# A two-layer residual kernel whose first layer is computed by one level of Strassen, with the second layer as a phase of its own

## The reference

```python
# layer 0: one weight matrix for all, plus a gated low-rank part
base   = einsum('btd,od->bto', x, W)                  # W: 1024 x 1024
logits = einsum('btd,ed->bte', x, Wr) + 5.0 * one_hot(language_id)   # 8 experts
topw, topi = top_k(logits, 2);  weights = softmax(topw)
gates  = sum(one_hot(topi) * weights)
h      = einsum('btd,erd->bter', x, A)                # 8 experts, rank 16
x = x + base + 2.0 * einsum('bter,bte,eor->bto', h, gates, B)
# layer 1: each sequence has its own 1024 x 1024 matrix, picked by adapter id
w = weight[adapter_ids]                               # 16 matrices to pick from
x = x + einsum('bsi,boi->bso', x, w)
```

## Time and profile before

| | |
|---|---|
| median of 3 runs | 424.41 us (424.09 to 424.89) |
| profiled execution, its own time from first to last instruction (the span) | 423.0 us |
| PE busy | 414.4 us, 98% of the span |
| DVE busy | 314.1 us, 74% |
| ACT busy | 163.1 us, 39% |
| POOL busy | 59.5 us, 14% |
| DMA traffic | 68.5 MB, mean 162 GB/s |
| granted TensorE clock | 1.000 |

### The profile page before, as it was taken

One profiled execution on the slowest core, in us unless ns is written; L12 is line 12 of the kernel. 1 busy time (PEld: TensorE's weight loads), 2 busy tenths in 40 slices (PEclk: granted clock), 3 DMA queues, 4 the chain that ended last, 5 costly groups with the idle time before them and its releaser, 6 DMA issues.

```text
span 423.0 us, 6707 instructions
## 1 busy us (share of the span) xinstructions
PE 414.4 (98%) x1978; PEld 349.1 (83%) x1978; DVE 314.1 (74%) x378; ACT 163.1 (39%) x192; POOL 59.5 (14%) x104
## 2 busy tenths in 40 slices
PE   8898999999999999999999999999999999999996
PEld 8786888888898888888888888888889888888885
DVE  3999999999307999998615799999830799994410
ACT  3432544555212455454321445455421245533321
POOL 1021211201200121012110022111310012221000
PEclk9999999999999999999999999999999999999999
DMA  7994677797913666699650576679960356654111
GB/s 173 232 219 120 167 190 200 212 259 203 225 47 99 150 187 180 161 260 249 173 132 0 153 181 188 170 218 252 243 160 26 99 151 175 189 161 123 51 50 50
DMA packets 82542, 68.52 MB, mean 162 GB/s; under 512 B 7986, under 2 KB 82258, under 8 KB 82514
## 3 DMA queue, kind: packets, MB, share of 16 engines
q1 hardware_dynamic: 65618, 59.84, 55.3%
q10 hardware_dynamic: 16896, 8.39, 7.3%
HBM read 59.81 MB, written 8.39 MB: 161 GB/s over the span
## 4 chain that ended last, share of the span: by engine, by line
PE 89%; DVE 3%; DMA 2%; SPq 2%; issue 2%; ACT 0%; POOL 0%; DVEq 0%; ACTq 0%; POOLq 0%
PE banks L564 28%; PE banks L565 28%; PE banks L566 28%; PE banks L577 4%; SPq L255 2%; PE banks L579 1%; DMA raw<-in_L_cond_W_dram 1%; DMA raw<-in_x_dram 1%; DVE turned L349 1%; DVE turned L345 0%; DVE w_lo L356 0%; POOL raw L301 0%; PE gT_ps L611 0%; ACT w_hi L487 0%; DVE gT_lo L449 0%
## 5 line engine op out<-in xcount | busy, mean ns | idle before, releaser
L356 DVE TENSOR_TENSOR w_lo<-turned,w_hi 128x1024 fp32r<-128x1024 f32 x96 | 118.8, 1259 | 38.8 <-ACT w_hi L487 38.0
L487 ACT ACTIVATE w_hi<-turned 128x1024 fp32r<-128x1024 f32 x96 | 101.5, 1062 | 113.1 <-DVE turned L349 103.3
L349 DVE STREAM_TRANSPOSE turned<-raw 128x1024 f32<-128x1024 f32 x113 | 135.3, 1225 | 10.1 <-DMA raw<-in_x_dram 5.1
L301 POOL TENSOR_TENSOR raw<-raw,ident 128x128 f32<-128x128 f32 x96 | 58.4, 608 | 325.9 <-DMA raw<-in_L_cond_weight_dram 182.7
L564 PE MATMUL banks<-xT_hi,w_hi 128*128 128x512 f32 x256 | 100.2, 391 | 0.0
L565 PE MATMUL banks<-xT_lo,w_hi 128*128 128x512 f32 x256 | 99.7, 389 | 0.0
L566 PE MATMUL banks<-xT_hi,w_lo 128*128 128x512 f32 x256 | 99.6, 389 | 0.0
L564 PE MATMUL banks<-w_hi,x1T_hi 128*128 128x512 f32 x256 | 99.6, 389 | 0.0
L565 PE MATMUL banks<-w_lo,x1T_hi 128*128 128x512 f32 x256 | 99.6, 389 | 0.0
L566 PE MATMUL banks<-w_hi,x1T_lo 128*128 128x512 f32 x256 | 99.6, 389 | 0.0
L566 PEld LDWEIGHTS banks<-xT_hi,w_lo 128*128 128x128 f32 x256 | 48.1, 188 | 10.0
(11 more groups left out here) (54 smaller groups left out, 197.8 us busy)
## 6 DMA issues: line engine op xcount, KB each, us to landing
raw<-in_L_cond_weight_dram SPq DMA_DIRECT2D x256, 128.0 KB, 2.7
raw<-in_L_cond_W_dram SPq DMA_DIRECT2D x128, 128.0 KB, 3.5
raw<-in_x_dram SPq DMA_DIRECT2D x64, 128.0 KB, 3.3
out_dram<-out_stage ACTq DMA_DIRECT2D x32, 256.0 KB, 3.1
raw<-in_L_cond_A_dram SPq DMA_DIRECT2D x4, 128.0 KB, 3.1
raw<-in_L_cond_B_dram SPq DMA_DIRECT2D x4, 128.0 KB, 4.5
gated<-in_L_cond_Wr_dram SPq DMA_DIRECT2D x4, 8.0 KB
lang_i<-in_itok_B_dram SPq DMA_DIRECT2D x1, 4.0 KB, 2.9
```

Of the source, the lines that this page charges most:

```text
L301: nc.gpsimd.tensor_tensor(spot, spot, ident[:].rearrange("p (q j) -> p q j", q=Q), ALU.add)\
L349: nc.vector.transpose(turned[:, slot(item, ch, last, 2)].rearrange("p m (q s) -> p q m s", q=Q), raw[:, s, :].rearrange("p (q m j) -> p q ...
L356: nc.vector.tensor_tensor(dest(False, item), turned[:, slot(item, ch, last, 2)], dest(True, item).bitcast(F32), ALU.subtract)\
L487: nc.scalar.activation(dest(True, item), turned[:, slot(item, ch, last, 2)], ACT.Copy)\
```

## The change

**Layer 0 by Strassen.** Tokens are worked in two spans of 1024 instead of four chunks of 512. In a span, x (two halves of 512 tokens, two halves of 512 features) and W (two halves of outputs, two of features) are 2 x 2 blocks, and seven products of sums stand for eight plain ones. A round computes 4 output tiles of 128 outputs x 512 tokens: seven `product`s, each 4 steps of three matmuls with 512 columns. There are 4 rounds in a span, 8 in all. Each operand part of a product is a piece: for x a piece for each tile of tokens (`("x", span, t, i)`), for W one for each round (`("u", n, i)`), each 128 x 512. Of the seven x pieces five are sums, of the seven W pieces five are sums; POOL makes them (`add_up`) into a ring of three half tiles. Every piece is then split by ACT and DVE as before. Partial results are combined by ACT copies, three DVE instructions and one POOL add in each round, and each round ends in the eviction of 4 banks by ACT and DVE.

**Features** are computed on the turned x itself (f32, one matmul of 136 columns for each step) in place of two fp32r matmuls on its split parts. The gates are made four times, for four tiles each.

**x1 by way of DRAM.** The results of layer 0, split in high and low parts, are stored to a DRAM scratch `x1_kept` by SP (`keep_round`) and loaded back for each sequence in layer 1 (`load_x1`).

**Layer 1** runs behind all of layer 0: 8 sequences (rows), each 4 banks of 8 steps of three matmuls with 512 columns. Its 64 weight tiles come through a ring of five raw tiles, four turned tiles and three groups of four tiles of split weights, in buffers that Strassen's operands leave.

The core of the diff, new lines:

```diff
+    ORDER = (4, 5, 2, 3, 1, 6, 7)
+    FIRST_ORDER = (4, 2, 5, 3, 1, 6, 7)
+    SUMMED_X = (1, 3, 4, 6, 7)
+    SUMMED_U = (1, 2, 5, 6, 7)
+    FRONT = ([("a",)] + [("x", 0, 0, t) for t in range(XT)] + [("w", 0, 1), ("w", 0, 0)] +
+             [("x", 0, 1, t) for t in range(XT)] + [("b",)])
+    LOADS = (FRONT + pair(1) + pair(2) + pair(3) + X_EARLY + pair(4) + X_LATE + pair(5) + pair(6) + pair(7))
+    RAW = 3
+    RAW1 = 5
+    PIECES_A = [[("x", 0, t, 2), ("x", 0, t, 4)] for t in range(XT)]
+    PIECES_W0 = [("u", 0, 4), ("u", 0, 2), ("u", 0, 5), ("u", 0, 3)]
+    PIECES_B0 = [("x", 0, 0, i) for i in (5, 3, 1, 6, 7)]
+    PIECES_B = [("x", 0, t, i) for t in range(1, XT) for i in (5, 3)]
+    PIECES_CROSS = {i: [("x", 0, t, i) for t in range(1, XT)] + [("u", 0, i)] for i in (1, 6, 7)}
+    def after_product(n, j):
...
+        own = [("x", 1, 0, i), ("x", 1, 1, i)] if n == HM - 1 else []
+        return own + [("u", n + 1, i)]
+    def late_pieces(i):
+        return [("x", 1, 2, i), ("x", 1, 3, i)]
...
+    x1_kept = nc.dram_tensor("x1_kept", [M, P, 2, NB * T], F32, kind="Internal").ap()
...
+            def load_x1(row):      # SP
...
+                else:
+                    sp.wait_ge(l1_ready, (row - 1) * 2 * TT)
...
+                for low in range(2):
+                    sp.dma_start(x1_part(row, low).bitcast(F32),
+                                 x1_kept[:, :, low, row * T:(row + 1) * T].rearrange("m p t -> p m t"))\
+                        .then_inc(x1_loaded[row % 2], 16)
...
+            load_x1(1)
+            keep_round(7)
+            for row in range(1, NB):
+                for m in range(M):
+                    load_w1(row * M + m, ids)
+                if row + 1 < NB:
+                    load_x1(row + 1)
...
+            def add_up(p):         # POOL
+                k = SUM_AT[p]
+                pool.wait_ge(transposed, needs(p))
+                if k >= SUM_SLOTS:
+                    pool.wait_ge(lo_done, PIECE_AT[SUMS[k - SUM_SLOTS]] + 1)
+                left, right, op = terms(p)
+                nc.gpsimd.tensor_tensor(sum_tile(p), left, right, op).then_inc(summed_up, 1)
...
+            turn(("w", 0, 1))      # DVE, first span
+            lows(PIECES_A[3])
+            lows(PIECES_W0[0:2])
+            turn(("w", 0, 0))
+            turn(("x", 0, 1, 0))
+            lows(PIECES_W0[2:4])
+            turn(("x", 0, 1, 1))
+            lows(PIECES_B0)
+            turn(("x", 0, 1, 2))
+            turn(("x", 0, 1, 3))
+            lows(PIECES_B)
+            lows(PIECES_CROSS[1])
+            make_u1(0)
             dve.wait_ge(setup, 4)
             make_gates(0)
+            lows(PIECES_CROSS[6])
+            make_g(0)
+            lows(PIECES_CROSS[7])
+            make_w1(0)
+            turn(("b",))
+            make_gates(1)
+            b_low()
+            for n in range(NR - 1):
+                for item in pair(n + 1):
+                    turn(item)
+                ...                # lows(after_product(n, 0)); four turns of x in round 2
+                if n:
+                    make_u1(n)
+                lows(after_product(n, 1))
+                lows(after_product(n, 2))
...
+                if n % HM == 0:
+                    gT_low(n // HM)
+                lows(after_product(n, 6))
+                evict(n)
+                if n == HM - 1:
+                    for item in X_LATE:
+                        turn(item)
+                    lows(late_pieces(4))
+                    lows(late_pieces(5))
+                    make_gates(2)
+                    lows(late_pieces(2))
+                    lows(late_pieces(3))
+                    lows(late_pieces(1))
+                    make_gates(3)
+                    lows(late_pieces(6))
+                    lows(late_pieces(7))
...
+            def round_of(n):       # PE
...
+                pe.wait_ge(u1_done, n + 1)
+                product(n, 3, bank(n, "12"), False)
+                if n % HM == 0:
+                    pe.wait_ge(gated_ready, n // HM * 2 + 1)
+                free(n, "11")
+                product(n, 1, bank(n, "11"), True)
+                if n == 0:
+                    turn_gated(0)
+                free(n, "22")
+                product(n, 6, bank(n, "22"), True)
+                if n % HM == 0:
+                    turn_gated(n // HM * 2 + 1)
+                pe.wait_ge(w1_done, n + 1)
+                product(n, 7, bank(n, "11"), False)
+                pe.wait_ge(gT_done, n // HM + 1)
...
+            features(0, 0)
+            for _ in range(FILL):  # 18 matmuls on the identity
+                nc.tensor.matmul(banks[:, 7, 0:P], ident[:], ident[:], start=True, stop=True)
+            product(0, 4, bank(0, "21"), True)
+            pe.wait_ge(s4_copied, 1)
+            product(0, 2, bank(0, "21"), False)
+            features(0, 1)
+            for n in range(HM):
+                round_of(n)
+            features(1, 0)
+            features(1, 1)
+            for n in range(HM, NR):
+                round_of(n)
```

More of the change, by code:

```diff
@@ new lines, in cond_resid_kernel, with summed @@
+    PIECES = ([p for l in PIECES_A for p in l] + PIECES_W0 + PIECES_B0 + PIECES_B +
+              PIECES_CROSS[1] + PIECES_CROSS[6] + PIECES_CROSS[7])
+    for n in range(NR):
+        PIECES += [p for j in range(7) for p in after_product(n, j)]
+        if n == HM - 1:
+            PIECES += [p for i in ORDER for p in late_pieces(i)]
+    PIECE_AT = {p: k for k, p in enumerate(PIECES)}
+    assert len(PIECE_AT) == len(PIECES) == SPANS * XT * 7 + NR * 7
+    def summed(p):
+        return p[3] in SUMMED_X if p[0] == "x" else p[2] in SUMMED_U
@@ L55, in cond_resid_kernel, with made @@
+    SUMS = [p for p in PIECES if summed(p)]
+    SUM_AT = {p: k for k, p in enumerate(SUMS)}
+    SUM_SLOTS = 3
+    def made(i, n):
+        return 7 * n + order(n).index(i) + 1
     GROUPS = 3
[L56 to L60, removed]
+    NW1 = NB * M
+    L1_OUTS = NB * 2 * TT
     OUTS = 4
[L62 to L68, removed]
@@ new lines, in x1_part, with turned @@
+        def x1_part(row, low):
+            at = low * XSIZE if row % 2 == 0 else 14 * XSIZE + low * XSIZE
+            return operands[:, at:at + XSIZE].rearrange("p (m f) -> p m f", m=M)
+        def turned(item):
+            if item[0] == "w":
+                return tiles[:, 3 + item[2]]
+            if item[0] == "b":
+                return tiles[:, 6]
+            _, s, half, t = item
+            if s == 0:
+                return tiles[:, 5 + t if half == 0 else (9, 10, 5, 9)[t]]
+            return tiles[:, 5 + 2 * (t % 2) + half]
@@ new lines, in needs, with source, dest @@
+        def needs(p):
+            if p[0] == "x":
+                _, s, t, i = p
+                return max(AT[("x", s, half, t)] for half in {2: (0,), 4: (0,), 3: (1,), 5: (1,)}.get(i, (0, 1))) + 1
+            _, n, i = p
+            return max(AT[("w", n, which)] for which in {2: (1,), 4: (1,), 3: (0,), 5: (0,)}.get(i, (0, 1))) + 1
+        def source(p):
+            return (sum_tile(p) if summed(p) else terms(p)[0]).rearrange("p (m f) -> p m f", m=HM)
+        def dest(p, low):
+            if p[0] == "x":
+                return x_part(p[3], low)[:, :, p[2] * P:(p[2] + 1) * P]
+            return u_part(p[2], low)
@@ new lines, in add_all, with add_v @@
+            def add_all(pieces):
+                for p in pieces:
+                    if summed(p):
+                        add_up(p)
+            def add_v(n):
+                pool.wait_ge(w1_done, n + 1)
+                pool.wait_ge(g_done, n + 1)
+                nc.gpsimd.tensor_tensor(w1_v, w1_v, f21_g, ALU.add).then_inc(v_done, 1)
+            for t in range(XT - 1):
+                add_all(PIECES_A[t])
+            add_ones(("w", 0, 1))
+            add_all(PIECES_A[XT - 1])
+            add_ones(("w", 0, 0))
@@ new lines, in _ @@
+            for n in range(3):
+                turn_w1(n)
+            make_u1(NR - 1)
+            turn_w1(3)
+            low_w1(0)
+            make_g(NR - 1)
+            low_w1(1)
+            turn_w1(4)
+            make_w1(NR - 1)
+            low_w1(2)
+            turn_w1(5)
+            low_w1(3)
+            turn_w1(6)
+            low_w1(4)
+            evict(NR - 1)
+            for n in range(7, NW1):
+                turn_w1(n)
+                low_w1(n - 2)
+            low_w1(NW1 - 2)
```

997 lines of the change are left out of this document (597 added, 400 removed).

## The result

The changed kernel takes 569.26 us (567.55 to 571.6, 4 runs) against 424.26 us before: a ratio of 1.341, 95% interval 1.337 to 1.345. Slower was forecast, but 462 us, with 436 to 490 as the range. The profiled execution has a span of 569.8 us, 109 more than the prediction's sum of 461.

What follows compares the result with a forecast made beforehand. PE's matmuls were taken to bound the kernel, with waits for its operands added: 390 without waits + 36 front + 17 between spans + 4 clock + 14 layer 1 = 461, so 462 us; range 436 to 490.

Steps and rivals of the forecast that it cites:

- The sign: Whole kernel: the change makes it slower, chance 0.91 (faster 0.07, same 0.02).
- the account of PE: PE: 96 fewer matmuls in layer 0 at 0.2267 us each, −21.8 us; 390 us in all without waits.
- the front: Start of layer 0 to the end of round 0: waits for pieces and gates cost 36 us, ending at 81.
- the border: Between the spans, rounds 3 to 4: late eviction, turns, lows and gates delay product 3, 17 us.
- POOL's sum: Layer 0, one 128 x 512 add on POOL: 1.6 us, bounds 0.46 and 2.3.
- Rival 1: Layer 0: pieces are made in time, neither front nor middle is late, −53 us, total 409 us; chance 0.08.
- Rival 3: Layer 1 bound by DMA at 233 to 260 GB/s, total 482 to 504 us; chance 0.18.
- The step that failed: Layer 1 priced as 49.3 MB at 290 GB/s: 192.4 us against 178.2 without waits, +14 us.
- DVE's subtract: Layer 0, DVE making the low part of one half-tile piece: 0.65 us.
- a plain round: Layer 0 round with 13.2 us of DVE and 11 us of POOL work, hidden behind PE's 21.8 us.
- The gates: Gate blocks on DVE, at the front and between the spans, delay PE's products: some 4.5 us each.
- The clock: PE restarting at a lower clock after long waits at the start of layer 0: +4 us, bounds 0 and 10.

Runs made afterwards that it cites:

- l1_no_reload: Changed kernel without the reload of x1 for rows 2 to 7 of layer 1 and its waits (omits needed work, pricing only): 515.5 us.
- no_sums: Changed kernel without the 80 sums on POOL, each summed piece taking its first term alone (omits needed work, pricing only): 526.4 us.
- l1_x1_act: Changed kernel with the reload of x1 for rows 2 to 7 issued by ACT instead of SP, same bytes: 532.9 us.
- l1_drain: Changed kernel with all low parts of a layer 1 row's weights made on DVE before the next row's first tile is turned: 536.3 us.

## Why the prediction was wrong

**Right.** The sign, and the account of PE: 96 matmuls fewer, and the longest runs without waits at PE's price (rounds 5 and 6 take 22.6 us each, 21.8 was worked out; the rows of `l1_no_reload` come every 21.8). A matmul of the features starts 0.23 us after the one before, where 0.21 was taken: 3 us for 128 of them. The three waits of the front are the three named, product 3 behind `make_u1(0)`, the second gates, `gT_low`, and the border is where it was put. POOL's sum was 1.54 for 1.6. Rival 1, pieces made in time, is refuted: `no_sums` gains 43 us. Rival 3 had nearly the rate of layer 1 (233 GB/s and up for 218 measured), but not the reason, since the same bytes go at 298.

**The step that failed: layer 1, +63 of 109 us.** The prediction wrote down the parts, SP's two large loads "which stand in the queue before the next row's weights and wait until PE has finished the row before", and then priced the stage by bytes over a rate, 49.3 MB at 290 GB/s. The rate was about right: 298 where nothing else holds. What was missed is that DVE's order ties the last low part of a row to the next row's second tile, and so PE's row to that wait. Cutting this chain at either end gave back 33 and 36 us with all bytes still moved; dropping the reload gave 54.

The distance from the start of row 1 to that of row 7 divides it: 187.2 us in the changed kernel, 147.9 in `l1_x1_act`, 130.6 in `l1_no_reload`, and six rows of PE's own 21.8 are 130.8. So 39 us go with the ring, some of them by way of the clock, and 17 with the bytes of the reload. The start of layer 1 adds some 20 over PE's own time: a wait of 5.4 us, one of 11.1 (at 344) and the slow matmuls behind them. The two waits stay in `l1_x1_act` (3.7 and 10.7) and `l1_no_reload` (4.7 and 9.8); `l1_drain` has 3.4 and 3.7. In all, layer 1 takes 77 us more than PE's own 178, where the prediction had 14. Bytes are the second limit, not the first.

**DVE's subtract, mis-sized: 0.65 taken, 1.06 measured.** The row was there: an add on POOL stretched from 0.46 to 0.78 beside a DVE subtract. I charged the contention to POOL alone, and by 0.1 us. It falls on both, and on DVE it is 42 us in all: each subtract that starts during a sum waits for the sum's end. By the trace some 19 of them lie before the end of round 0, 9 in round 3 and 8 at the border and in round 4: the front (+12) and the border with round 3 (+19). How these 31 us divide between DVE's longer subtract and other causes wasn't measured one by one; `no_sums`, which removes the contention and POOL's sums together, takes 22 us out of the front and 17 out of the border.

**Round 2, forecast as a plain round: +15.** The prediction counted DVE's work there and called it hidden. It did not follow the loads of x for the four turns, though the turns stand before `make_u1(2)`. Part was the queue (−5 with the stores moved), part the place of the turns (−6); what the ring of three raw tiles takes was not measured by itself.

**The gates** were put on the path at 4.5 us each in four places; leaving them out gives 11 us, not 18. **The clock** was put at +4, for the front: filling the waits of layer 0 gained nothing, and the cost is in layer 1, some 15 us by the estimate above, for which the prediction had no term.

**Two slips on the rows.** 128 x 0.24 is 30.7, not 30.3, which moves a bound by 0.4 us. And 307 GB/s is not the best 2 us of the trace of before: 210 to 212 us holds 329. Neither changes the forecast.

**Left open.** How the 12 and 19 us of the front and the border divide, what the clock costs in layer 1 when the ring stays, and whether a deeper ring of raw tiles would free round 2: none of these has a run of its own.

## What to carry to other kernels

Where a stage is priced by bytes over bandwidth, follow one item first through every in-order list that it passes: if a lag of two in one engine's order reaches into the next block, and that block's load waits for this block's end, the stage runs at the latency of the loop, although bandwidth is free (218 of 298 GB/s used here). And a wait of PE can cost more than its length, when the matmuls behind it start at the lower clock and lie on the same path. An algorithm that saves an eighth of half of the matmuls (22 us here) pays only if its operands come at no one's cost; here 80 sums, six instructions in each round that combine partial results and a trip of x1 through DRAM left the kernel 180 us above the 390 us of PE's own work. A wait that goes when one instruction is moved often comes back one round later; price such an edit by the whole time, not by the wait.

## What the runs showed of the hardware

- A DVE subtract with two SBUF inputs (128 x 512) that starts while a POOL sum of the same size runs ends 0.55 to 0.58 us after the sum (55 of 112), and a POOL sum that starts during such a subtract ends 1.12 to 1.16 us after it (52 of 80). Apart from each other they take 0.72 and 1.28 us. In the two runs whose POOL does only the identity adds and eight combinations the subtract took 0.70 and 0.75 on average.
- The DMA engines held 298 GB/s for 140 us with runs of 1 KB and 512 bytes mixed, at a summed share of 1.12. In the trace of before 1.01 went with 260 GB/s; a share near 1 had not been the limit.
- In the changed kernel PE stood idle from 368.0 to 376.0 us. The granted clock was 0.50 from 371.7 to 381.8 us and 1.00 from 381.9 to 405.6. That is 1.2 and 2.4 GHz: the matmuls of 512 columns start 0.43 us apart in the first stretch and 0.23 in the second. With the waits of layer 0 filled the clock read 1.00 at the same places of the program where it had read 0.74, and the kernel took the same time.
